# A fused attention and gated-recurrence kernel: softmax products one slot later, and the last residual added by accumulating DMAs

## The reference

```python
def attn(x):                       # x: (8, 4096, 1024), 16 heads of 64
    q, k, v = x @ Wq.T, x @ Wk.T, x @ Wv.T      # each split as (N, heads, S, 64)
    att = softmax(einsum('nqhd,nkhd->nhqk', q, k) / 8, axis=3)
    ...
```

```python
x = x + layernorm(attn(layernorm(x)) @ Wo.T + bo)          # first residual, "x1" below
# recurrence over the 8 images, c starts at in_c
f, i = sigmoid(ln(x) @ wf.T + c @ uf.T + bf), sigmoid(ln(x) @ wi.T + c @ ui.T + bi)
c = f * c + i * tanh(ln(x) @ wc.T + c @ uc.T + bc)
h = tanh(ln(x) @ wo.T + c_final @ uo.T + bo)
out = x + layernorm(h)                                      # second residual
```

## Time and profile before

| | before |
|---|---|
| median of 3 runs | 1463.65 us |
| the profiled execution's own time | 1466.65 us |
| its span on the slowest core (core 5) | 1465.1 us |
| spans of the 8 cores | 1442.2 to 1465.1 us |
| PE busy | 1330.1 us, 91% of the span |
| DVE, ACT, POOL busy | 809.7, 560.7, 421.0 us |
| granted TensorE clock, core 5 | 0.966 of full speed |

### The profile page before, as it was taken

How to read it: one execution, slowest core, us unless ns; L and a number is a source line. 1 busy time by engine, 2 the same in 40 slices (tenths; PEclk the granted TensorE clock), 3 DMA queues, 4 the chain that set the end, 5 groups by cost and what they waited for, 6 DMA issues and landing times.

```text
span 1465.1 us, 25930 instructions; the slowest of 8 cores (1442.2 to 1465.1 us)
## 1 busy us (share of the span) xinstructions
PE 1330.1 (91%) x8256; PEld 741.3 (51%) x8256; DVE 809.7 (55%) x1447; ACT 560.7 (38%) x1570; POOL 421.0 (29%) x887
## 2 busy tenths in 40 slices
PE   4777998889787888989999999999999999999993
PEld 2546675656555555765444444444444444444441
DVE  3346776766757666556554454535445453225774
ACT  1225565454554545445422222222222222212564
POOL 4013444444454434222211010100101010001887
PEclk9899999999999999999999999999999999999997
DMA  9964777757665675583562222222313211009784
GB/s 197 159 113 112 143 137 165 159 124 162 143 175 121 171 150 132 181 298 126 182 216 86 73 86 102 86 87 87 97 62 99 74 58 72 1 8 340 262 293 189
DMA packets 126372, 202.52 MB, mean 138 GB/s; under 512 B 72704, under 2 KB 78848, under 8 KB 123136
## 3 DMA queue, kind: packets, MB, share of 16 engines
q1 hardware_dynamic: 110256, 175.71, 38.3%
q0 software_dynamic: 15984, 25.17, 12.6%
HBM read 158.91 MB, written 83.89 MB: 166 GB/s over the span
## 4 chain that ended last, share of the span: by engine, by line
PE 62%; DMA 10%; DVE 8%; POOL 8%; issue 6%; SPq 3%; ACT 1%; POOLq 1%; DVEq 0%; ACTq 0%
PE ps_big L425 10%; PE ps_s L425 10%; PE ps_big L413 10%; PE ps_s L413 10%; POOL pn L905 5%; PE ps_big L300 4%; PE ps_big L326 3%; PE ps_big L309 3%; SPq L1009 3%; PE ps_big L288 3%; DMA v_scr<-vtok 2%; DMA wv<-wvT 2%; PE ps_o L483 2%; PE ps_s L483 2%; PE ps_big L483 2%
## 5 line engine op out<-in xcount | busy, mean ns | idle before, releaser
L807 ACT ACTIVATE p<-ps_s,nm 128x128 f32<-128x128 f32 x512 | 182.0, 371 | 249.3 <-DVE nm L576 248.8
L905 POOL TENSOR_SCALAR pn<-p,rl 128x128 bf16<-128x128 f32 x512 | 180.5, 369 | 241.6 <-DVE rl L572 238.4
L583 DVE STREAM_TRANSPOSE pt<-pn 128x512 bf16<-128x512 bf16 x128 | 90.9, 710 | 129.4 <-POOL pn L905 125.5
L288 PE MATMUL ps_big<-wv,xT 128*128 128x512 bf16 x512 | 126.8, 394 | 12.4 <-ACT vtok L791 11.0
L300 PE MATMUL ps_big<-xT,wq 128*128 128x256 bf16 x1024 | 131.5, 285 | 6.6 <-DVE qst L568 4.9
L300 PE MATMUL ps_big<-xT,wk 128*128 128x256 bf16 x1024 | 124.2, 276 | 10.3 <-DMA wk<-wkT 8.2
L326 PE MATMUL ps_big<-wo,zT 128*128 128x512 bf16 x512 | 125.6, 390 | 1.5 <-DVE kst L566 0.9
L644 DVE SCALAR_TENSOR_TENSOR ti<-ti,tg 128x512 f32<-128x512 f32 x64 | 44.2, 691 | 140.6 <-ACT tg L856 140.6
L300 PEld LDWEIGHTS ps_big<-xT,wq 128*128 128x128 bf16 x1024 | 102.0, 102 | 23.0 <-issue 8.1
L300 PEld LDWEIGHTS ps_big<-xT,wk 128*128 128x128 bf16 x1024 | 98.6, 99 | 24.3 <-issue 11.5
L807 ACT ACTIVATION_READ_ACCUMULATOR p<-ps_s,nm 128x1 f32 x512 | 106.9, 209 | 0.0
(11 more groups left out here) (154 smaller groups left out, 2395.6 us busy)
## 6 DMA issues: line engine op xcount, KB each, us to landing
z_scr<-zb SPq DMA_DIRECT2D x32, 512.0 KB, 7.0
h<-x_scr SPq DMA_DIRECT2D x32, 512.0 KB, 5.7
out<-h SPq DMA_DIRECT2D x32, 512.0 KB, 3.3
xin<-x SPq DMA_DIRECT2D x28, 512.0 KB, 5.8
zb<-z_scr SPq DMA_DIRECT2D x24, 512.0 KB, 4.0
xrb<-xr SPq DMA_DIRECT2D x24, 512.0 KB, 3.8
x_scr<-xrb SPq DMA_DIRECT2D x24, 512.0 KB, 2.9
vst<-v_scr SPq DMA_DIRECT2D x64, 128.0 KB, 7.6
```

Of the source, the lines that this page charges most:

```text
L288: mm = t.matmul(bank[:], xT[n % 2][:, ft * 512 + i * 128:ft * 512 + (i + 1) * 128], wv[:, ft * D + half * 512:ft * D + half * 512 + 512], ...
L583: v.transpose(pt[G % 2][:], pn[G % 2][:]).then_inc(s_tr, 1)
L807: ex = a.activation(p32[G % 2][:, c], psS[G % 2][:, c], AF.Exp, bias=nm[G % 2][:, pk:pk + 1], accum_out=ls[G % 2][:, pk:pk + 1])
L905: op = g.tensor_scalar(pn[G % 2][:, c], p32[G % 2][:, c], rl[G % 2][:, pk:pk + 1], 1.0, AL.mult, AL.mult)
```

## The change

Two parts. In the attention slots DVE's transpose goes from slot G-1 to slot G-2 and PE's `values` from G-2 to G-3, with `oevict`, the early-post steps, the load of V blocks and the `rstd1` step moved by zero to two slots to match; `precast` goes behind the other work of POOL's slot. In the output stage the scratch `x1_scr` is gone: the first residual is stored straight to the output tensor, and `h_out` is no longer an addition on POOL but a DMA issued by POOL that adds `hbuf` into the output in DRAM. `hbuf` has 10 tiles in place of 6 and is freed by that DMA's landing; `h1`, its loads and SP's stores are gone.

```diff
@@ tensor
-            if G >= 2:
-                values(G - 2)
+            if G >= 3:
+                values(G - 3)
...
+        values(NG - 3)
+        w_part(1, 0)
         values(NG - 2)
-        w_part(1, 0)
+        w_part(1, 1)
         values(NG - 1)
-        w_part(1, 1)
@@ vector
-            if 1 <= G <= NG:
-                ptrans(G - 1)
+            if 2 <= G <= NG + 1:
+                ptrans(G - 2)
...
-                if G % 8 == 2:
+                if G % 8 == 3:
                     post_stats(e)
...
-                if half == 0 and w >= 6:
-                    v.wait_ge(h_po, w - 5)
+                if half == 0 and w >= NH:
+                    v.wait_ge(d_ho[w % NH], 16 * (w // NH))
@@ scalar
-            if 32 <= G < 96 and G % 8 == 3:
+            if 32 <= G < 96 and G % 8 == 4:
                 post_norm((G - 32) // 8)
-            if 2 <= G < NG + 2 and G % 2 == 1:
-                oevict((G - 2) // 2)
+            if G >= 4 and G % 2 == 0:
+                oevict((G - 4) // 2)
@@ gpsimd
-            if G < 96 and G % 3 == 1:
-                precast(G // 3)
-            if G < NG and n < 6 and s % 4 == 0:
+            if G < NG and n < 6 and s % 4 == 1:
                 rstd1((n + 2) * 4 + s // 4)
             if 32 <= G < 96:
-                if G % 8 == 2:
+                if G % 8 == 4:
                     post_r1(e)
-                elif G % 8 == 4:
+                elif G % 8 == 5:
                     g.wait_ge(p_n1, e + 1)
                     g.tensor_tensor(exr[:], exr[:], ez[:], AL.add).then_inc(p_x1, 1)
-                elif G % 8 == 6:
+                elif G % 8 == 7:
                     post_r2(e)
+            if G < 96 and G % 3 == 1:
+                precast(G // 3)
...
         def h_out(w):
             g.wait_ge(h_ap, w + 1)
-            g.wait_ge(d_h1[w % 12], 16 * (w // 12 + 1))
-            g.tensor_tensor(h1[w % 12][:], h1[w % 12][:], hbuf[w % 6][:], AL.add).then_inc(h_po, 1)
+            g.dma_start(out=out_d[n * 4 + tt], in_=hbuf[w % NH][:],
+                        accum_op=AL.add).then_inc(d_ho[w % NH], 16)
...
         for w in range(36):
+            if w >= 4:
+                h_out(w - 4)
             if w % 2 == 0 and 2 <= w <= 32:
                 h_rstd(w // 2 - 1)
-            if w >= 4:
-                h_out(w - 4)
@@ sync
-            s.dma_start(out=x1_scr[u], in_=exr[:]).then_inc(d_ex1, 16)
+            s.dma_start(out=out_d[u], in_=exr[:]).then_inc(d_ex1, 16)
...
-                if (G + 6) % 4 == 0 and 3 <= (G + 6) // 4 < 32:
-                    vload((G + 6) // 4)
+                if (G + 5) % 4 == 0 and 3 <= (G + 5) // 4 < 32:
+                    vload((G + 5) // 4)
...
-            if 32 <= G < 96:
+            if 33 <= G <= 96:
-                if G % 8 == 0:
+                if G % 8 == 1:
                     early_load(e)
-                elif G % 8 == 5:
+                elif G % 8 == 6:
                     early_x1_store(e)
-                elif G % 8 == 7:
-                    early_xl_store(e)
+                elif G % 8 == 0:
+                    early_xl_store(e - 1)
...
-        for w in range(32):
-            s.wait_ge(h_po, w + 1)
-            s.dma_start(out=out_d[n * 4 + tt], in_=h1[w % 12][:]).then_inc(d_ho[w % 12], 16)
-            if w >= 2 and w - 2 + 12 < 32:
-                h1_load(w - 2 + 12)
```

More of the change, by code:

```diff
@@ L212, in build @@
     hbuf = [at(f"hbuf{i}", [128, D], F32, o) for i, o in
-            enumerate((oXZ, oXZ + 4096, oXLN, oXZ + 8192, oXZ + 12288, oP + 8192))]
-    h1 = [at(f"h1_{i}", [128, D], F32, (oK0, oQ1, oK1)[i // 4] + 4096 * (i % 4))
-          for i in range(12)]
+            enumerate((oXZ, oXZ + 4096, oXLN, oXZ + 8192, oXZ + 12288, oP + 8192,
+                        oK0, oK0 + 4096, oK0 + 8192, oK0 + 12288))]
+    NH = len(hbuf)
     hx = {5: at("hx5", [128, 4096], BF16, oWV), 4: at("hx4", [128, 4096], BF16, oWV + 8192),
@@ L251, in build @@
     d_hx = [sem(f"d_hx{i}") for i in range(6)]
-    d_h1 = [sem(f"d_h1_{i}") for i in range(12)]
-    d_ho = [sem(f"d_ho{i}") for i in range(12)]
+    d_ho = [sem(f"d_ho{i}") for i in range(NH)]
     s_ms, s_cst = sem("s_ms"), sem("s_cst")
@@ L266, in build @@
     s_h, h_ev, h_th, h_bs, h_bn = (sem(n) for n in ("s_h", "h_ev", "h_th", "h_bs", "h_bn"))
[L267 removed]
+    h_r, h_m, h_mn, h_ap = (sem(n) for n in ("h_r", "h_m", "h_mn", "h_ap"))
     ZLAST = {u: BN[("Z", u // 4, u % 4, 1)] for u in range(32)}
@@ L968, in h_out @@
         def h_out(w):
+            n, tt = 7 - w // 4, w % 4
             g.wait_ge(h_ap, w + 1)
-            g.wait_ge(d_h1[w % 12], 16 * (w // 12 + 1))
-            g.tensor_tensor(h1[w % 12][:], h1[w % 12][:], hbuf[w % 6][:], AL.add).then_inc(h_po, 1)
+            g.dma_start(out=out_d[n * 4 + tt], in_=hbuf[w % NH][:],
+                        accum_op=AL.add).then_inc(d_ho[w % NH], 16)
+        g.wait_ge(d_x1[0], 16 * 12)
+        g.wait_ge(d_x1[1], 16 * 12)
+        g.wait_ge(d_ex1, 16 * 8)
         for w in range(36):
+            if w >= 4:
+                h_out(w - 4)
             if w % 2 == 0 and 2 <= w <= 32:
                 h_rstd(w // 2 - 1)
-            if w >= 4:
-                h_out(w - 4)
+        for i in range(NH):
+            g.wait_ge(d_ho[i], 16 * len(range(i, 32, NH)))
     def sync(s):
```

36 lines of the change are left out of this document (8 added, 28 removed).

## The result

The change runs in 1446.36 us (median of 4 runs, 1440.83 to 1449.18), against 1465.64 us for the kernel before on the same chip: a ratio of 0.9862, 95% interval 0.9825 to 0.9900. That is 20 us faster (15 to 26 by the interval), where 63 were forecast. Ratios here are always to the kernel before on the same chip, and they leave out the executions in which the cores of a die ran slower at a lower granted clock, while the medians in us beside them count these too. The profiled execution took 1445.23 us; its slowest core is core 0, span 1443.7 us, clock 0.968.

A forecast was written before the change was run, and what follows sets the result against it. The prediction took PE to bound most stages, and DVE's wait for POOL before the transpose to bound images 2 to 5. Its sum was 1466.65 - 53.9 - 9.2 = 1403.5, given as 1403 us, range 1383 to 1438.

The forecast's parts named there:

- the transposes' wait: Attention images 2 to 5: DVE's 89.6 us wait for POOL's normalising before the transpose should go nearly whole.
- the 53.9 us: Attention images 2 to 5: saving from the later transpose, 337.9 us down to 284 (ends -72.7 and -24.2).
- The early loads are issued a slot later, and their reader comes a slot later too: 0.: Attention: moving issue and reader of the early residual's loads by one slot each was to cost nothing.
- 71 us an image: Attention images 2 to 5: image 1's 66.3 us plus two thirds of 6.9 us extra DVE work.
- V stores 0, plus or minus 8: Attention: shorter slots against SP's first V store no longer behind the `exl` wait, set at 0, plus or minus 8 us.
- Images 0, 1, 6 and 7: 0: Attention: images 0, 1 and 7 taken as PE-bound already, image 6 as 0 to -2; no gain counted.
- Part 2, -9.2 us: Output stage: residual added by DMA instead of POOL ends the kernel at 1455.9, not 1465.1 us (-11.8 to -4.6).
- the forecast of the last landing: Output stage: last accumulating DMA lands 14 to 18 us behind PE's last matmul.
- 2.7 us of DMA time a tile: Output stage: an accumulated tile costs the DMA engines what its load and store cost, under PE's 3.45 us.
- the lagging queue: Output stage rival, chance 0.10: accumulating DMAs take 3.85 to 5 us a tile; whole time 1416 to 1451 us.
- the slow one: Output stage rival, chance 0.10: accumulating packets wait for DRAM reads, 6.9 us a tile; whole time 1510 us.
- A second wait takes its place: Attention rival, chance 0.18: waits for exponentials, V stores or early loads leave only 24.2 us gained there; whole time 1433 us.

The follow-up runs named there:

- exl_own: The changed kernel with `exl` in 2 KB of its own, no longer lying over `ez`: 1452.26 us, ratio 0.9885.
- early_s0: The changed kernel with the early loads put back in slot 0, directly behind the store of `exl`: 1426.48 us, ratio 0.9728.
- part2: The output-stage half of the change alone, on the kernel before, attention slots untouched: 1466.75 us, ratio 0.9980.
- waits_on_sp: The changed kernel with the closing waits for the accumulating DMAs moved from GpSimd's stream to SyncE's: 1443.96 us, ratio 0.9851.
- early_add_dve: The changed kernel with own-space `exl`, early loads in slot 0, last four tiles stored plainly, early residual added by VectorE (last edit): 1398.03 us, ratio 0.9501.
- best_order: The changed kernel with own-space `exl`, slot-0 early loads, last four tiles stored plainly, VectorE's last additions held for GpSimd's last deviation: 1417.46 us, ratio 0.9635.

## Why the prediction was wrong

It had the sign, and 1403 us where 1446 came out: above the range, too.

**What bounds the kernel, and the transposes' wait.** Right. The wait of 89.6 us went whole, and the recurrence did not move. But the next wait took back what it freed in images 2 to 5, all but 12 to 15 of the 53.9 us.

**"The early loads are issued a slot later, and their reader comes a slot later too: 0."** This is the step that failed, and with it the -53.9 us. I counted slots between issue and reader, and those did stay equal. Two things make a slot on SyncE's queue longer than one on VectorE's. The loads had stood directly behind the store of `exl`. A slot later they stand behind an `xin` load that waits for VectorE to be through with `xln`, so the reader's own engine holds them back. And each slot became shorter, while the landings became longer: 10.8 us in place of 6.9 for `exr`, 7.3 in place of 3.5 for `exl` (medians). `exl_own` and `early_s0` show that place and landing both bind: the place alone brings 1.3% (part of it perhaps by the shorter landing that came with it), the landing alone nothing, both together 2.4%. In the forecast's own terms SP's queue was to be a gain there, since the first V store no longer stands behind the wait for `exl`; what was queued behind the other waits of SP I did not price.

**71 us an image.** Size nearly right, for partly wrong reasons. With the loads mended images 2 to 5 take 72.6 on average (290.3), with the last edit 69.3. What lies between is a cost that I did not know: the change put GpSimd's early addition into the slot of `xln`, 1.9 us eight times. I had treated VectorE's 56.7 us as fixed.

**V stores 0, plus or minus 8.** Right: 14.3 us in the change against 20.6, and 21.6 where the images are short.

**Images 0, 1, 6 and 7: 0.** Wrong, to the good. I took image 1 to be TensorE's already and image 0 to be like it. Over eight cores image 0 became 6.1 us shorter, image 1 1.6, image 6 2.7, and what follows up to TensorE's last matmul 2.0 longer. By luck, then, more than a third of what the change brought comes from stages that I had put at nothing; without it the miss would be larger. `precast` was not tried alone.

**Part 2, -9.2 us.** The mechanism was right and the size wrong: -1.1 us in the two slowest cores' traces (-0.7 by the medians over eight), -2.9 in the comparison of `part2`. Two terms. From TensorE's last matmul to the last issue I had 8.0 us and it is 9.8: two issues of 0.9 us, one ahead of the last deviation and one ahead of the last issue, were not in the sum. The landing, 7.8 taken from the casting DMAs, is 8.1 at most. So the forecast of the last landing, 14 to 18 us behind TensorE, held (17.9). What I took for the end was not the end: GpSimd's drain of 5.2 us behind it was in no view I had read. In the kernel before it ran beside the last store; with the landings awaited on GpSimd itself it follows them.

**2.7 us of DMA time a tile.** Too low: 3.41. It lies between the bounds (1.4 and 3.85) and just under TensorE's 3.45, so the DMA engines had 1% to spare, and neither the lagging queue nor the slow one came. The Trainium skill (Collectives: The Full Stack, The bandwidth ceiling) gives the adding phase of a collective half the rate of the copying one, for its two source reads. By that rule a tile would cost two plain ones, 2.6 us. This queue doesn't agree: the addition makes a tile 2.6 times as dear as a plain store (3.41 against 1.30).

**The rivals.** "A second wait takes its place" is what came, and it named the early loads among three candidates. I priced it at 1433 and gave it 0.18. Against it I had set image 1, at 66.3 us with a DMA share of 0.70. Image 1 has no early loads, so it said nothing about a wait for them. The mark I had given for it, images near 78 us with another engine's wait in the transposes' place, fits: 77.2 to 82.1.

## What to carry to other kernels

When steps are shifted together, don't compare their distance in slots: write down for each issuing queue what stands ahead of a moved DMA afterwards and whose progress that waits for, and set the landing, in microseconds, against the new, shorter slots. A buffer and a place in a queue can hide each other, so a mend that brings nothing alone is to be tried with the other. And read what the last engine does behind its last piece of work: here, waiting on GpSimd for its last DMAs put that engine's drain of 5 us behind them. Compare stages over all cores before giving a difference to chance.

## What was unexpected in the hardware

- An accumulating DMA of 512 KB costs the 16 DMA engines 3.41 us, a plain one on the same queue 1.30. GpSimd needs 894 against 596 ns to issue it, and it lands in 6.5 against 3.0 us. The engines' share is 0.94 at 141 GB/s in that stage.
- GpSimd's closing drain takes 5.1 to 5.2 us when it starts behind the landings, and in `waits_on_sp`, where it starts ahead of the last one, it still ends 2.3 us beyond it. SyncE's takes 7 ns in `waits_on_sp`.
- VectorE and GpSimd hold each other up over whole instructions: `xln` takes 2.69 us beside GpSimd's two-operand addition and 0.77 to 1.04 without it (`early_add_dve`), and GpSimd's two tiny steps take 2.54 us beside VectorE's additions and 0.93 without them (`best_order`). The Trainium skill (SBUF — State Buffer, SBUF: two separate sides) calls the port pair that the two share an exclusive lock and not a split of bandwidth. The traces agree: `xln` ends 0.56 us behind the addition that it met. In the profile such a wait doesn't show as idle time but as a longer busy instruction, and only the mean of the line gives it away.
